# Attention's first batch: the order of the split of x, the masks, the out bias and the weight splits

## The chip, the cores and the metric

The kernel runs on one core of one Trainium2 chip. A core has five engines with a queue each: TensorE (PE, matrix products and transposes), VectorE (DVE), ScalarE (ACT), GpSimd (POOL) and SyncE (SP, which issues transfers here). They meet only at semaphores. The metric is the device time of one execution in microseconds, as the median of several runs.

## The reference

Four layers in a row over x, of shape (8, 512, 512): a stencil, an attention block, a feed-forward block and a gate. Only the attention block bears on the change:

```
scale, shift = split(silu(sin_emb(timestep)) @ W_ada + b_ada)
x = layernorm(src) * (1 + scale) + shift
q, k, v = (x @ Wq + bq), (x @ Wk + bk), (x @ Wv + bv)      # 16 heads of 32
scores = q k^T / sqrt(32) + attention_bias                  # 8 x 16 x 512 x 512
scores = where(src_mask, -inf, scores)
ctx = softmax(scores) @ v
x = x + (ctx @ Wo + bo)
```

All is float32. The attention bias is an input of 134 MB and is read from HBM pair by pair.

## The kernel before

The phases follow each other with a barrier between them: `stencil`, `attention`, `feed_forwards`. In attention a batch is 64 units (`NU`), one per head and block of 128 queries; 16 units (`UC`) make a chunk `c` of four heads, four units with the same queries a group. Each engine has a list written out by hand: first a head for batch 0, then `body`, once for each batch, which walks `u` over the units and says at which unit each side task stands. Nothing reorders the lists.

Precision comes from splits: a float32 tensor is copied to a rounded high part (`...H`, on ACT) and the rest to a low part (`...L`, on DVE), and a product is three matrix products (`split_matmul`, L94 to L98). For the four weight matrices, numbered 0 to 3 (Wq, Wk, Wv, Wo), these are `weights_high(k)` (L872) and `weights_low(k)` (L1135), 128 x 2048 elements each. Staging places are two: Wv comes to the place of Wq (`y`, a shared tile that later holds probabilities) and Wo to that of Wk (the second x). SP issues Wv's load when `s_wl`, the count of low parts, is at least 1, and Wo's at 2, with the bias load of pair 3 behind.

The head of batch 0, engine by engine:

- POOL: identity, loads of the small biases, `power(0)` (var to the power -0.5, L777, then a small product L779), the two halves of the mask (`make_mask`, uint8 to -3e38 or 0, L809), the mask added to bias pairs 0 to 2 (`add_mask`, L815; a pair is two heads of one block, 128 x 1024), and `out_bias` for four row blocks (L798).
- ACT: high parts of weights 0 and 1, `xhat` for four row blocks (L883, waits for the power), `x_high` for four column blocks (L878), `q_high`, `k_high`, high part 2, `copy_v`, the first `exp` (L907), high part 3.
- DVE: statistics, low part 0, the four row blocks times `scale` (L1223) and plus `shift` (L1226), `bq` scaled, `x_low` for four blocks (L1153), low part 1, `q_low`, `k_low`, low part 2, `copy_vT`, two sums of scores (L1180), low part 3.
- PE: four groups of four transposes of x (L992), projections q, k and v ("w" in the code) of chunk 0, the transposition of v, the first four scores (L1046).

PE's results lie in eight banks. `bank_of` gives x two of them in the head, `pS[0]` and `pJ[1]`, in turn, and `first_bank` makes the third and fourth transposition wait for `x_low` of an earlier one (`s_xl`):

```
waits = {("x", 2): (s_xl, 1), ("x", 3): (s_xl, 3), ("k", C): (s_xl, 2), ("w", C): (s_ql, 1), ("v", 0): (s_kl, 1)}
```

In `body`, `exp(u + 1)` and `sum_scores(u + 2)` are issued at unit `u`, and `add_mask` works three pairs ahead. `add_part`, which adds the projected context to x, is the first reader of the out bias's result, in chunk 1. `project_y`, in chunk 1, is the first reader of Wo's parts.

## Time and profile before

| | us |
|---|---|
| median of three runs | 2770.02 |
| lowest, highest | 2769.93, 2770.68 |
| profiled execution | 2768.22 |
| its span | 2766.3 |

PE is busy 2639.3 us of the span, 95%, DVE 1697.8 (61%), ACT 1024.1 (37%), POOL 1025.2 (37%). In the granted clock of PE, 0.981 of 2.4 GHz over the span, the places at half of it are few. Attention begins at 205.5 us of the span and ends near 1190. A row of a timeline says start, duration, engine, line, operation, what is written and read, and in brackets how long the engine was idle before and what ended that. Starts are from the beginning of the span.

### The profile page before, as it was taken

The page shows a single profiled execution, that of the slowest core. Times are in us where ns is not written, and L with a number is a line of the kernel's source. Part 1 is how long each engine was busy: PE and PEld are TensorE (multiplying, and loading weights), DVE is VectorE, ACT ScalarE, POOL GpSimd, SP SyncE. Part 2 cuts the span into 40 slices and gives each one's busy share as a digit, 9 for nine tenths or more (in the row PEclk, how much of TensorE's full clock was granted, in tenths as well). Part 3 has the DMA queues.
Part 4 walks back from the last instruction along what each step waited for, and adds up shares of the span by engine and source line. Part 5 has one row for each costly group of instructions (what it writes and reads, how often), then busy time and mean ns, then how long its engine had stood idle before and what let it go on. Part 6 is the DMA issues. An engine that isn't in the chain of part 4 may idle for free. (4 is left out here: it accounts for less than half of the span.)

```text
span 2766.3 us, 46266 instructions
## 1 busy us (share of the span) xinstructions
PE 2639.3 (95%) x17072; PEld 2037.0 (74%) x17088; DVE 1697.8 (61%) x3341; ACT 1024.1 (37%) x2160; POOL 1025.2 (37%) x756
## 2 busy tenths in 40 slices
PE   7975999999999999969999999999999999999997
PEld 2434777777777777657888888888787887888775
DVE  9976777777777777756444444445554564565443
ACT  1114666666666666611111111111223232322222
POOL 1005677776777777533100110012222322322210
PEclk9997999999999999989999999999999999999998
DMA  4234564655646555531111011103333343244311
GB/s 173 107 132 128 164 194 139 188 154 180 189 144 188 145 185 164 153 105 54 31 31 31 1 31 31 31 1 124 115 103 106 111 134 125 89 130 126 104 46 38
DMA packets 212972, 305.99 MB, mean 111 GB/s; under 512 B 14604, under 2 KB 93516, under 8 KB 210064
## 3 DMA queue, kind: packets, MB, share of 16 engines
q1 hardware_dynamic: 211662, 301.99, 35.3%
q8 instruction: 138, 2.26, 0.3%
q0 software_dynamic: 1088, 1.05, 0.2%
q14 instruction: 84, 0.69, 0.1%
HBM read 268.94 MB, written 34.04 MB: 110 GB/s over the span
## 5 line engine op out<-in xcount | busy, mean ns | idle before, releaser
L815 POOL TENSOR_TENSOR at_bias<-at_bias,at_mask 128x1024 f32<-128x1024 f32 x224 | 483.0, 2160 | 247.3 <-DMA at_bias<-in_fside_Bx16xSxS 245.9
L1180 DVE CUSTOM_DVE_ANT_0 at_bias<-at_bias,at_bank_score 128x512 f32<-128x512 f32 x512 | 338.4, 682 | 186.9 <-PE at_bank_score L1046 140.3
L96 PE MATMUL ff_bank_out<-ff_WH,ff_gH 128*128 128x512 f32 x1024 | 407.9, 398 | 1.9 <-DVE ff_gL L1939 1.9
L96 PE MATMUL ff_bank_hid<-ff_hH,ff_WH 128*128 128x512 f32 x1024 | 402.2, 393 | 2.8 <-DVE ff_WL L1892 2.8
L1667 ACT ACTIVATE ff_g<-ff_bank_hid,ff_b1c 128x512 f32<-128x512 f32 x256 | 175.5, 686 | 607.7 <-PE ff_bank_hid L98 607.7
L98 PE MATMUL ff_bank_out<-ff_WH,ff_gL 128*128 128x512 f32 x1024 | 400.3, 391 | 0.0
L97 PE MATMUL ff_bank_out<-ff_WL,ff_gH 128*128 128x512 f32 x1024 | 399.9, 391 | 0.0
L97 PE MATMUL ff_bank_hid<-ff_hL,ff_WH 128*128 128x512 f32 x1024 | 399.8, 390 | 0.0
L98 PE MATMUL ff_bank_hid<-ff_hH,ff_WL 128*128 128x512 f32 x1024 | 399.7, 390 | 0.0
L1939 DVE TENSOR_TENSOR ff_gL<-ff_g,ff_gH 128x512 fp32r<-128x512 f32 x256 | 178.7, 698 | 348.9 <-ACT ff_g L1667 344.4
L1566 POOL TENSOR_SCALAR ff_WH<-shared 128x1024 fp32r<-128x1024 f32 x144 | 177.1, 1230 | 568.9 <-PE ff_bank_out L98 330.5
L907 ACT ACTIVATE shared<-at_bias,at_nmax 128x512 f32<-128x512 f32 x512 | 366.5, 717 | 17.7 <-DVE at_nmax L1180 17.7
L1053 PE MATMUL at_bank_probT<-at_ident,shared 128*128 128x128 f32 x2048 | 313.8, 280 | 6.1 <-ACT shared L907 6.1
L1053 PEld LDWEIGHTS at_bank_probT<-at_ident,shared 128*128 128x128 f32 x2048 | 228.4, 141 | 94.3 <-issue 67.7
L1937 DVE CAST ff_gH<-ff_g 128x512 fp32r<-128x512 f32 x128 | 72.4, 566 | 359.7 <-ACT ff_g L1667 359.6
L1666 ACT ACTIVATE ff_gH<-ff_bank_hid,ff_b1c 128x512 fp32r<-128x512 f32 x128 | 88.3, 690 | 519.0 <-PE ff_bank_hid L98 519.0
L915 ACT ACTIVATE at_probT<-at_bank_probT 128x512 f32<-128x512 f32 x256 | 152.9, 597 | 269.6 <-PE at_bank_probT L1053 158.4
L96 PEld LDWEIGHTS ff_bank_hid<-ff_hH,ff_WH 128*128 128x128 f32 x1024 | 193.0, 188 | 45.2 <-DVE ff_WL L1892 3.6
L98 PEld LDWEIGHTS ff_bank_out<-ff_WH,ff_gL 128*128 128x128 f32 x1024 | 192.9, 188 | 41.0
L98 PEld LDWEIGHTS ff_bank_hid<-ff_hH,ff_WL 128*128 128x128 f32 x1024 | 192.9, 188 | 40.7
L96 PEld LDWEIGHTS ff_bank_out<-ff_WH,ff_gH 128*128 128x128 f32 x1024 | 193.3, 189 | 39.5 <-DVE ff_gL L1939 2.3
L97 PEld LDWEIGHTS ff_bank_hid<-ff_hL,ff_WH 128*128 128x128 f32 x1024 | 192.9, 188 | 39.6
(310 smaller groups left out, 4282.2 us busy)
## 6 DMA issues: line engine op xcount, KB each, us to landing
at_bias<-in_fside_Bx16xSxS SPq DMA_DIRECT2D x256, 512.0 KB, 3.8
shared<-in_L_cond_Wi SPq DMA_DIRECT2D x128, 256.0 KB, 2.9
shared<-in_L_cond_Wo SPq DMA_DIRECT2D x128, 256.0 KB, 3.0
shared<-x_after_layer SPq DMA_DIRECT2D x64, 256.0 KB, 5.2
st_f<-in_x SPq DMA_DIRECT2D x8, 1024.0 KB, 6.9
x_after_attention<-shared SPq DMA_DIRECT2D x32, 256.0 KB, 2.3
shared<-x_after_attention SPq DMA_DIRECT2D x32, 256.0 KB, 4.4
shared<-in_L_cond_W SPq DMA_DIRECT2D x32, 256.0 KB, 3.0
```

The costliest lines, as they stand in the source:

```text
L96: pe.matmul(out, wh, xh, start=first, stop=False)
L97: pe.matmul(out, wh, xl, start=False, stop=False)
L98: return pe.matmul(out, wl, xh, start=False, stop=last)
L815: pool.tensor_tensor(bias[i % NB][:, :, :], bias[i % NB][:, :, :], mask[:, i // 2 % R, :].unsqueeze(1).to_broadcast([P, 2, S]), ALU.add).t ...
L907: act.activation(prob[u % 2][:, :], bias[u // 2 % NB][:, u % 2, :], ACT.Exp, scale=-1.0, bias=nmax[:, u % 4:u % 4 + 1], accum_out=sums[:, ...
L915: act.activation(probT[g % 2][:, j].rearrange("p k q -> p (k q)"), pT[0][:, :], ACT.Copy).then_inc(s_pt[0], 1)
L1053: t = pe.transpose(pT[u % 2][:, k * P:(k + 1) * P], prob[u % 2][:, k * P:(k + 1) * P], ident[:, :])
L1180: dve.tensor_tensor_reduce(t, t, pS[u % HC][:, :], -1.0, 3.0e38, ALU.add, ALU.min, nmax[:, u % 4:u % 4 + 1]).then_inc(s_max, 1)
L1566: pool.tensor_scalar(WH[:, f, :], stage[f % 2][:, :], 1.0, 0.0, ALU.mult, ALU.add).then_inc(s_wh, 1)
L1666: act.activation(gH[f % 2][:, :], pg[f % 2][:, :], func, bias=column).then_inc(s_gh, 1)
L1667: act.activation(g32[f % 2][:, :], pg[f % 2][:, :], func, bias=column).then_inc(s_g32, 1)
L1939: dve.tensor_tensor(gL[f % 2][:, :], g32[f % 2][:, :], f32(gH[f % 2][:, :]), ALU.subtract).then_inc(s_g, 1)
```

## The change

Only the head and the first batch's body change.

- POOL: only the first half of the mask is made behind the power. Then POOL waits for all of `x_low` (`s_xl` at 4), adds the mask to pairs 0 to 2, and makes the second half. The four `out_bias` of batch 0 go into the body, at units 8, 10, 12 and 14.
- DVE: low part 0 goes behind the `shift` additions, low part 2 from behind `k_low` to ahead of `q_low`, low part 3 into the body at unit 11.
- ACT: high part 2 goes ahead of `q_high`, high part 3 into the body at unit 9.
- PE: the first transposes of x use four banks, `pS[0]`, `pJ[1]`, `pT[0]`, `pT[1]`, and wait for no `x_low`.

```diff
+        first_x = (pS[0], pJ[1], pT[0], pT[1])
+        def x_bank(n, m):
+            return first_x[m] if is_first(n) else bank_of("x", m)
...
             def out_bias(n, slot, r):
                 if r == 0:
+                    pool.wait_ge(s_const, 64)
                     pool.wait_ge(s_xp, n * C + C)
...
             power(0)
-            for half in range(2):
-                make_mask(0, half)
+            make_mask(0, 0)
+            pool.wait_ge(s_xl, C)
             for i in range(3):
                 if i not in ON_PE:
                     add_mask(0, i)
-            pool.wait_ge(s_const, 64)
-            for r in range(R):
-                out_bias(0, 0, r)
+            make_mask(0, 1)
...
+                    if is_first(n) and u in (8, 10, 12, 14):
+                        out_bias(0, 0, (u - 8) // 2)
...
             act.wait_ge(s_const, 64)
+            weights_high(2)
             act.wait_ge(s_bq, 1)
             q_high(0, 0)
             k_high(0, 0)
-            weights_high(2)
             copy_v(0, 0)
             exp(0, 0)
-            weights_high(3)
...
+                    if is_first(n) and u == 9:
+                        weights_high(3)
...
-                waits = {("x", 2): (s_xl, 1), ("x", 3): (s_xl, 3), ("k", C): (s_xl, 2), ("w", C): (s_ql, 1), ("v", 0): (s_kl, 1)}
+                waits = {("k", C): (s_xl, 2), ("w", C): (s_ql, 1), ("v", 0): (s_kl, 1)}
...
             mean_var(0)
-            weights_low(0)
...
+            weights_low(0)
             for m in range(C):
                 x_low(0, 0, m)
             weights_low(1)
+            weights_low(2)
             dve.wait_ge(s_bq, 1)
             q_low(0, 0)
             k_low(0, 0)
-            weights_low(2)
             copy_vT(0, 0)
             sum_scores(0, 0)
             sum_scores(0, 1)
-            weights_low(3)
...
+                    if is_first(n) and u == 11:
+                        weights_low(3)
```

DVE's queue in the head, before (`at_WL` are the low parts of the weights, `shared` the rows of x, `at_xL` the low part of x):

```order
L1135 TENSOR_TENSOR at_WL<-shared,at_WH 128x2048
L1223 TENSOR_TENSOR shared<-shared,at_scale 128x512 x4
L1226 TENSOR_TENSOR shared<-shared,at_shift 128x512 x4
L1228 TENSOR_SCALAR at_bc<-at_bc 128x4
L1153 TENSOR_TENSOR at_xL<-at_bank_score,at_xH 128x512
L1153 TENSOR_TENSOR at_xL<-at_bank_proj,at_xH 128x512
L1153 TENSOR_TENSOR at_xL<-at_bank_score,at_xH 128x512 x2
L1135 TENSOR_TENSOR at_WL<-shared,at_WH 128x2048
L1158 SCALAR_TENSOR_TENSOR at_qL<-at_bank_proj,at_bc,at_qH 128x512
L1164 SCALAR_TENSOR_TENSOR at_kL<-at_bank_proj,at_bc,at_kH 128x512
L1135 TENSOR_TENSOR at_WL<-shared,at_WH 128x2048
L1192 TENSOR_SCALAR at_vT<-at_bank_proj,at_bc 128x512
```

And of the change, whose lines are 5 to 7 further down:

```order
L1229 TENSOR_TENSOR shared<-shared,at_scale 128x512 x4
L1232 TENSOR_TENSOR shared<-shared,at_shift 128x512 x4
L1234 TENSOR_SCALAR at_bc<-at_bc 128x4
L1142 TENSOR_TENSOR at_WL<-shared,at_WH 128x2048
L1160 TENSOR_TENSOR at_xL<-at_bank_score,at_xH 128x512
L1160 TENSOR_TENSOR at_xL<-at_bank_proj,at_xH 128x512
L1160 TENSOR_TENSOR at_xL<-at_bank_probT,at_xH 128x512 x2
L1142 TENSOR_TENSOR at_WL<-shared,at_WH 128x2048 x2
L1165 SCALAR_TENSOR_TENSOR at_qL<-at_bank_proj,at_bc,at_qH 128x512
L1171 SCALAR_TENSOR_TENSOR at_kL<-at_bank_proj,at_bc,at_kH 128x512
L1199 TENSOR_SCALAR at_vT<-at_bank_proj,at_bc 128x512
```

The first low part moved behind the rows of x, the third ahead of q's and k's.

ACT's queue from the first rows of x to its first exps, before (`at_WH` are the high parts of the weights, L907 the exps):

```order
L883 ACTIVATE shared<-shared,at_mrstd,at_rstd 128x512 x4
L878 ACTIVATE at_xH<-at_bank_score 128x512
L878 ACTIVATE at_xH<-at_bank_proj 128x512
L878 ACTIVATE at_xH<-at_bank_score 128x512 x2
L888 ACTIVATE at_qH<-at_bank_proj,at_bc 128x512
L893 ACTIVATE at_kH<-at_bank_proj,at_bc 128x512
L872 ACTIVATE at_WH<-shared 128x2048
L898 ACTIVATE at_v<-at_bank_proj 128x512
L907 ACTIVATE shared,at_sums<-at_bias,at_nmax 128x512
L872 ACTIVATE at_WH<-shared 128x2048
L907 ACTIVATE shared,at_sums<-at_bias,at_nmax 128x512
```

And of the change:

```order
L889 ACTIVATE shared<-shared,at_mrstd,at_rstd 128x512 x4
L884 ACTIVATE at_xH<-at_bank_score 128x512
L884 ACTIVATE at_xH<-at_bank_proj 128x512
L884 ACTIVATE at_xH<-at_bank_probT 128x512 x2
L878 ACTIVATE at_WH<-shared 128x2048
L894 ACTIVATE at_qH<-at_bank_proj,at_bc 128x512
L899 ACTIVATE at_kH<-at_bank_proj,at_bc 128x512
L904 ACTIVATE at_v<-at_bank_proj 128x512
L913 ACTIVATE shared,at_sums<-at_bias,at_nmax 128x512 x2
```

The third high part stands ahead of q's and k's, and the fourth has left this stretch.

POOL's queue from the power on, before (L809 the halves of the mask, L815 masked pairs, L798 out bias):

```order
L777 TENSOR_TENSOR at_rstd<-at_var,at_mhalf 128x4
L779 TENSOR_TENSOR at_mrstd<-at_mneg,at_rstd 128x4
L809 TENSOR_SCALAR at_mask<-at_m 128x1024 x2
L815 TENSOR_TENSOR at_bias<-at_bias,at_mask 128x1024 x3
L798 TENSOR_TENSOR shared<-shared,at_bob 128x512 x4
L815 TENSOR_TENSOR at_bias<-at_bias,at_mask 128x1024 x10
```

And of the change:

```order
L782 TENSOR_TENSOR at_rstd<-at_var,at_mhalf 128x4
L784 TENSOR_TENSOR at_mrstd<-at_mneg,at_rstd 128x4
L815 TENSOR_SCALAR at_mask<-at_m 128x1024
L821 TENSOR_TENSOR at_bias<-at_bias,at_mask 128x1024 x3
L815 TENSOR_SCALAR at_mask<-at_m 128x1024
L821 TENSOR_TENSOR at_bias<-at_bias,at_mask 128x1024 x5
L804 TENSOR_TENSOR shared<-shared,at_bob 128x512
L821 TENSOR_TENSOR at_bias<-at_bias,at_mask 128x1024
L804 TENSOR_TENSOR shared<-shared,at_bob 128x512
```

The out bias stands between masked pairs of the batch now, and the three first pairs wait for the split of x.

## Rows read from the trace of the kernel before

**Rows 1.** Busy time by stretch: us, per engine, then PE's granted clock, DMA share, GB/s.
```profile
218.00:225.00 7.00, 0.00 (x0) 0.00 (x0) 7.00 (x6) 0.00 (x0) 5.00 (x2) 0.50 0.11 44
...
243.80:248.70 4.90, 4.87 (x12) 3.79 (x12) 0.00 (x0) 0.00 (x0) 1.87 (x1) 0.50 0.00 0
...
340.00:360.00 20.00, 20.00 (x219) 15.32 (x218) 14.87 (x36) 14.33 (x36) 16.33 (x12) 1.00 0.49 155
```

**Rows 2.** Waits, 190 to 300: who waited for whom, us, times, longest.
```profile
PE at_bank_score L992 <- DVE shared L1226: 32.8, 1, 32.8
```

**Rows 3.** Timeline of POOL, the head: start, us, engine, line, operation.
```profile
209.60 2.98 POOL L777 TENSOR_TENSOR at_rstd<-at_var,at_mhalf 128x4 f32<-128x4 f32 x1
...
212.95 1.04 POOL L809 TENSOR_SCALAR at_mask<-at_m 128x1024 bf16<-128x1024 uint8 x1
...
215.40 2.54 POOL L815 TENSOR_TENSOR at_bias<-at_bias,at_mask 128x1024 f32<-128x1024 f32 x1
...
233.03 3.34 POOL L798 TENSOR_TENSOR shared<-shared,at_bob 128x512 f32<-128x512 f32 x1
```

**Rows 4.** Timeline of DVE, the head.
```profile
209.38 2.30 DVE L1135 TENSOR_TENSOR at_WL<-shared,at_WH 128x2048 fp32r<-128x2048 f32 x1 [0.59 <-ACT at_WH L872]
...
215.89 2.60 DVE L1223 TENSOR_TENSOR shared<-shared,at_scale 128x512 f32<-128x512 f32 x1
...
224.67 0.68 DVE L1226 TENSOR_TENSOR shared<-shared,at_shift 128x512 f32<-128x512 f32 x1
```

**Rows 5.** Lines L777, L815, L798 of POOL, all executions: ns min/median/max.
```profile
L777 POOL TENSOR_TENSOR at_rstd<-at_var,at_mhalf x8: 1020/1022/2977, 209.6 to 1003.6; 128x4 f32<-128x4 f32 x8
...
L815 POOL TENSOR_TENSOR at_bias<-at_bias,at_mask x224: 2123/2147/3836, 215.4 to 1169.9; 128x1024 f32<-128x1024 f32 x112
...
L798 POOL TENSOR_TENSOR shared<-shared,at_bob x32: 1284/1295/3344, 231.8 to 1061.5; 128x512 f32<-128x512 f32 x32
```

**Rows 6.** Timeline of ACT, the head.
```profile
209.25 1.89 ACT L872 ACTIVATE at_WH<-shared 128x2048 fp32r<-128x2048 f32 x1
...
212.90 0.81 ACT L883 ACTIVATE shared<-shared,at_mrstd,at_rstd 128x512 f32<-128x512 f32 x1 [1.75 <-POOL at_mrstd L779]
```

**Rows 7.** Transfers issued from 205 to 260: KB each, us from issue to landing.
```profile
shared<-in_L_cond_Wv SPq DMA_DIRECT2D x1, 1024.0 KB, 8.4
...
at_bob<-in_L_cond_bo POOLq DMA_DIRECT2D x1, 256.0 KB, 7.6
...
shared<-in_L_cond_Wo SPq DMA_DIRECT2D x1, 1024.0 KB, 5.2
```

**Rows 8.** Timeline of PE, from the first transposes to the second of probabilities.
```profile
225.50 1.09 PE L992 MATMUL at_bank_score<-at_ident,shared 128*128 128x128 f32 x4 [32.82 <-DVE shared L1226]
226.38 1.06 PE L992 MATMUL at_bank_proj<-at_ident,shared 128*128 128x128 f32 x4
...
231.30 0.78 PE L96 MATMUL at_bank_proj<-at_xH,at_WH 128*128 128x512 f32 x1
...
243.83 0.76 PE L96 MATMUL at_bank_proj<-at_xH,at_WH 128*128 128x512 f32 x1 [4.99 <-DVE at_WL L1135]
...
255.91 1.12 PE L1053 MATMUL at_bank_probT<-at_ident,shared 128*128 128x128 f32 x4 [1.39 <-ACT shared L907]
```

**Rows 9.** Timelines of ACT, POOL, DVE and PE, first batch, units 10 to 16.
```profile
271.32 0.72 ACT L907 ACTIVATE shared<-at_bias,at_nmax 128x512 f32<-128x512 f32 x1
...
272.45 2.15 POOL L815 TENSOR_TENSOR at_bias<-at_bias,at_mask 128x1024 f32<-128x1024 f32 x1 [0.79 <-DMA at_bias<-in_fside_Bx16xSxS]
...
272.63 1.09 PE L1053 MATMUL at_bank_probT<-at_ident,shared 128*128 128x128 f32 x8
...
274.72 0.68 DVE L1180 CUSTOM_DVE_ANT_0 at_bias<-at_bias,at_bank_score 128x512 f32<-128x512 f32 x1
...
277.19 0.71 ACT L907 ACTIVATE shared<-at_bias,at_nmax 128x512 f32<-128x512 f32 x1
...
278.31 0.51 PE L1046 MATMUL at_bank_score<-at_kH,at_qH 32*128 32x512 f32 x4 [1.15 <-ACT shared L923]
```

More of the change, by code:

```diff
@@ L877, in x_high @@
                     wait_count(act, s_wp, (n - 1) * C)
-                act.activation(xH[slot][:, m, :], bank_of("x", m)[:, :], ACT.Copy).then_inc(s_xh, 1)
+                act.activation(xH[slot][:, m, :], x_bank(n, m)[:, :], ACT.Copy).then_inc(s_xh, 1)
             def xhat(n, slot, r):
@@ L1073, in _ @@
             for m in range(C):
-                transpose_x(0, 0, m, first_bank("x", m))
+                transpose_x(0, 0, m, x_bank(0, m))
             for kind in "qkw":
@@ L1152, in x_low @@
                 dve.wait_ge(s_xh, n * C + m + 1)
-                dve.tensor_tensor(xL[slot][:, m, :], bank_of("x", m)[:, :], f32(xH[slot][:, m, :]), ALU.subtract).then_inc(s_xl, 1)
+                dve.tensor_tensor(xL[slot][:, m, :], x_bank(n, m)[:, :], f32(xH[slot][:, m, :]), ALU.subtract).then_inc(s_xl, 1)
             def q_low(n, c):
```

## The prediction

> **What bounds the kernel now.** I read first the busy time by stretch, then what TensorE (PE) waits for, then each engine's rows in time order between the start of attention and its first scores.
>
> In the middle of attention's first batch PE is busy 20.00 of 20 us at full clock [rows 1]: from there on PE sets the pace, and work that starts earlier on PE ends the program earlier. Ahead of it PE stands still. It waits 32.8 us for the last addition of `shift` to x (`L1226`) [rows 2], and another 4.99 us, ahead of v's projection at 243.83, for the third weight split (`L1135`) [rows 8]. In the stretch 218 to 225 VectorE (DVE) is busy for all of 7.00 us and GpSimd (POOL) for 5.00, while PE and ScalarE (ACT) do nothing [rows 1]. So the end of the program hangs on a chain: power on POOL, four normalisations on ACT, eight row operations on DVE, transposes, split of x, projections q, k, v, first scores.
>
> Two things in the chain are dear for a reason that the rows show. The power takes 2.98 us here and 1.02 in the median of its eight executions [rows 3, 5]; the DVE split of the first weights (209.38, 2.30 us) lies over it [rows 4]. And the DVE rows of x take 2.60 us while POOL adds masks at 2.54 a pair, but 0.68 once POOL has finished [rows 3, 4].
>
> **The chain of after, step by step, in the times of this trace.** ACT is the next late one behind the power: `xhat` needs rstd, and ACT is in the second high part until 209.25 + 1.89 = 211.14 [rows 6]. A power of 1.02 ends at 210.62, the small product by about 210.95, so `xhat` starts at 211.1 and not 212.90. That is 1.8 us gained of the 1.96 that the power loses. The four `xhat` come 0.71 apart (each row is 0.81 long with its start overlapped), so DVE gets the first at 211.9 and the last at 214.1.
>
> DVE's eight row operations cost 0.61 each where POOL is silent (the row of 0.68 overlaps the one ahead). The fourth scaling starts when the last `xhat` is there, 214.1; then four shifts: 214.1 + 5 x 0.61 = 217.2. One mask conversion of 1.04 is still ahead of the wait on POOL [rows 3]. It would start at 210.95 if its bytes are there; the trace only says that they are by 212.95. So it costs DVE 0 to 1.0; I take 0.2, because the first scalings wait for `xhat` anyway. The vectors and biases that DVE asks for next are loaded from POOL's queue ahead of 209.60 and land within 7.6 us [rows 3, 7], by 217.2: nothing is added. First transpose at 217.4 against 225.50 [rows 8]: **8.1 us gained**.
>
> Transposes now go to four banks. At half clock four of them took 0.88 us (225.50 to 226.38 [rows 8]), so all four groups end by 217.4 + 3.5 = 220.9 and q can begin; before it was 231.30. Gain at this point 10.4. DVE does weights 0 first (217.4 to 219.7), then the four low parts of x; the last high part is ready about 221.8, its low part by 222.5. q's last step needs that and comes at 224 or later, so the split of x is out of the way; q ends between 223.7 and 226.
>
> Here the change adds **a wait that gates others**. Wv's load waits for weights 0 to be split, which is now at 219.7 instead of 211.7. A load of 1 MB took 8.4 us to land amid four others, and 5.2 with one behind it [rows 7]. I take 5.2, since nothing is under way then: landing at 224.9. On ACT the third high part (1.9, as long as the second [rows 6]) now stands ahead of q and k high, so they are queued behind this load: 224.9 to 226.8. On DVE weights 1 run from 222.4 to 224.7 and weights 2 stand ahead of q and k low.
>
> And the masks come in just here. POOL starts them when the last low part is made, 222.5. Weights 1 hold it off until 224.7, as weights 1 before stretched an addition of the out bias from 1.29 to 3.34 us [rows 3, 5]. Then mask pair 0 ends at about 226.8 and pair 1 starts at once, a moment ahead of weights 2. By the alternation of the 2.60 and 2.54 rows, weights 2 wait until about 228.9 and end at 231.1; q low ends at 231.8, and v's projection, which needs its bank and these weights, starts at **231.9 against 243.83** [rows 8]: 11.9 gained. With the 0.2 of the mask, **11.7**.
>
> The Trainium skill, SBUF — State Buffer, section Who interferes with whom, says that a DVE instruction with two SBUF inputs and a GpSimd instruction that reads SBUF exclude each other for the whole instruction. By that rule weights 2 wait out a whole mask pair and v starts at 231.9; without it they would not, and v would start at 229.8. The trace agrees (2.60 against 0.68).
>
> v's twelve products ran at half clock, busy 4.87 us for twelve [rows 1]; at full clock they would take half. PE idled 4.99 us ahead of them [rows 8] and will idle about 4 now, so I keep half clock: nothing gained, up to 2.4 kept for the range.
>
> **Fourth split inside the batch.** At the head it cost this: ACT's 1.9 between the first and second exp held the second transposition of probabilities, with 1.39 us idle at 255.91 [rows 8], and DVE's 2.3 held the third sum. Gone, PE comes to q's next step right after two transpositions: 1.6 us gained. Inside the batch it is paid again. ACT's next exp before was at 271.32 [rows 9]; with 1.9 in front it is at 273.2 and ends at 273.9; its transposition, the second half of PE's row at 272.63, began near 273.05, so PE loses about 1.1. This stretch has no slack to give it back: at 278.31 PE waits 1.15 us for ACT [rows 9]. DVE's 2.3 stand behind the sum of unit 13 and ahead of a copy and the sum of unit 14. That sum ends at 274.72 + 0.68 and its exp starts at 277.19 [rows 9], 1.8 later, and ACT is 1.1 late itself: 2.9 hide the 2.3. If a mask pair holds the port first, 2.1 more, PE loses 1.5. I take 1.8 for both, ends 1.1 and 4.2 (1.9 + 2.3, nothing hidden). The net of the fourth split is -1.6 + 1.8 = **0.2 lost**.
>
> **Out bias inside the batch.** Four POOL additions of 1.29 at units 8 to 14, each behind a mask pair of 2.15 [rows 3, 5]: POOL waited 0.79 us for the load at the pair of 272.45 [rows 9], so each pair falls 0.5 us back, 2.0 in all, while pairs are made three ahead of their use. Nothing is added; the upper end is 4 x 1.29 = 5.2, if POOL's lag reached the sums. The result is needed a chunk later. At the head it lay beside ACT and DVE work, and nothing waited for it there, so nothing comes back.
>
> **Sum.** -11.7 + 0.2 = -11.5 us. The profiled execution took 2768.2 with its span of 2766.3; its own after is 2756.7. It stands 1.8 under the median of the runs, 2770.02, and the runs are what is compared: 2770.0 - 11.5 = **2758.5**.
>
> **Rivals.** *A, luck at the port and the clock.* The high part is a little early, or mask pair 1 a little late, so weights 2 go ahead and v starts 2.1 earlier; PE's shorter pauses keep full clock in v, 1 to 2 more. For it: the two requests are only 0.1 us apart. Against: each needs its own chance. -11.5 - 2.1 - 1 = -14.6: 2755.4. *B, the load is the bound.* Wv takes 8.4 us as before; high part to 230.0, q and k high, and weights 2 behind mask pair 2: v at about 234.1. Against: the DMA engines are empty then. -9.3: 2760.7; with the fourth split at its dear end -6.9: 2763.1. *C, the batch gives it back.* If the first batch is paced by its bias loads and masks and not by PE, then an early start is waited out: PE's 20.00 of 20 speaks against it; within 2 us of before, 2769. *D, slower.* One mechanism, POOL in the batch: with out bias and the fourth split at the port, masks fall behind and sums stop. Its price is 5.2 for the out bias, 2.3 x 2 for the split's hold-ups of POOL and the pair behind, and 4.2 for the fourth split, 14.0; it decides once this exceeds the 13.3 gained ahead of it: 2770.7, and slower than before by over 0.2% only where more pairs follow late, 2776. Against it: POOL's idle 0.79 us. *E, the power isn't what the weight split slows*, say a first-use cost: then `xhat` starts at 212.9, all shifts by 1.8, 2760.3.
>
> **How the numbers follow.** Forecast with its bounds 0.52, A 0.16, B 0.13, E 0.07, C 0.08, D 0.04. The likeliest time is 2758.5. Leaving out C, D and the far ends of A and B gives 2755.0 to 2763.5. About 0.2% (5.5 us) is what a measurement of this kernel can tell from no change: faster by more is forecast, A, E and nearly all of B, 0.87; within it C, a rest of B and the mild end of D, 0.10; slower the rest of D, 0.03.
>
> **What would show it.** In the profile of after: power near 1.0 us; eight DVE row operations of 0.7; first transpose near 217.4 and four groups in 3.5 us with no wait for x low; third high part on ACT starting near 225 with a DMA as its releaser, q high behind it; third weight split on DVE near 229 to 231; v's projection near 232. Inside the batch: PE waiting about 2 us more between units 10 and 16. Wrong would be: x rows still slow (another cause than POOL), the third high part after 228 (load), or an unchanged time of PE's first batch end though its start moved 11 us (another bound).

## The result, and the profile after

| | before | after |
|---|---|---|
| median of five runs, us | 2770.02 | 2755.15 |
| lowest, highest | 2769.63, 2771.24 | 2753.82, 2758.74 |
| profiled execution | 2768.22 | 2754.93 |
| its span | 2766.3 | 2753.1 |
| granted clock of PE | 0.981 | 0.985 |

The ratio is 0.9948, with an interval of 0.9938 to 0.9959: faster by 0.5%, 14.9 us of the medians against 11.5 forecast. That is inside the range, though only 0.15 above its lower end of 2755.0, and nearer to rival A's 2755.4 than to the likeliest 2758.5; which of the two the trace shows is told below. The engines do the same work in less time. PE's line of the page of after (busy us, share, instructions):

```profile
PE 2635.7 (96%) x17088; PEld 2032.8 (74%) x17088; DVE 1697.2 (62%) x3341; ACT 1024.8 (37%) x2160; POOL 1024.8 (37%) x756
```

Timeline of GpSimd (POOL), after, against [rows 3]; a group "x3" is three instructions in a row:

```profile
209.47 1.04 POOL L782 TENSOR_TENSOR at_rstd<-at_var,at_mhalf 128x4 f32<-128x4 f32 x1
...
211.22 1.04 POOL L815 TENSOR_SCALAR at_mask<-at_m 128x1024 bf16<-128x1024 uint8 x1 [0.42 <-DMA at_m<-in_mask_Bx1xSxS_bk]
222.24 10.35 POOL L821 TENSOR_TENSOR at_bias<-at_bias,at_mask 128x1024 f32<-128x1024 f32 x3 [9.98 <-DVE at_xL L1160]
...
255.62 1.30 POOL L804 TENSOR_TENSOR shared<-shared,at_bob 128x512 f32<-128x512 f32 x1
256.87 2.15 POOL L821 TENSOR_TENSOR at_bias<-at_bias,at_mask 128x1024 f32<-128x1024 f32 x1
258.96 3.33 POOL L804 TENSOR_TENSOR shared<-shared,at_bob 128x512 f32<-128x512 f32 x1
```

The power is 1.04 us (2.98 before). The three masked pairs start when the last low part of x is there and take 10.35 us, not 3 x 2.15: they meet weight splits.

VectorE (DVE), after, against [rows 4]:

```profile
211.82 2.78 DVE L1229 TENSOR_TENSOR shared<-shared,at_scale 128x512 f32<-128x512 f32 x4 [3.17 <-ACT shared L889]
214.52 2.48 DVE L1232 TENSOR_TENSOR shared<-shared,at_shift 128x512 f32<-128x512 f32 x4
...
222.07 2.28 DVE L1142 TENSOR_TENSOR at_WL<-shared,at_WH 128x2048 fp32r<-128x2048 f32 x1
226.72 3.88 DVE L1142 TENSOR_TENSOR at_WL<-shared,at_WH 128x2048 fp32r<-128x2048 f32 x1 [2.37 <-ACT at_WH L878]
...
257.60 3.56 DVE L1142 TENSOR_TENSOR at_WL<-shared,at_WH 128x2048 fp32r<-128x2048 f32 x1
```

Eight row operations take 5.2 us together. The third weight split stands at 226.72 and takes 3.88, the fourth, now in the batch, 3.56: each waits behind a masked pair.

ScalarE (ACT), after:

```profile
224.78 1.92 ACT L878 ACTIVATE at_WH<-shared 128x2048 fp32r<-128x2048 f32 x1 [3.34 <-DMA shared<-in_L_cond_Wv]
226.60 0.67 ACT L894 ACTIVATE at_qH<-at_bank_proj,at_bc 128x512 fp32r<-128x512 f32 x1
```

The third high part waits for Wv's transfer, and q's high part is queued behind it, as the prediction said. PE, after, against [rows 8] and [rows 9]:

```profile
217.15 1.09 PE L999 MATMUL at_bank_score<-at_ident,shared 128*128 128x128 f32 x4 [24.46 <-DVE shared L1232]
...
231.32 0.50 PE L96 MATMUL at_bank_proj<-at_xH,at_WH 128*128 128x512 f32 x1 [3.81 <-DVE at_qL L1165]
...
237.42 0.51 PE L1053 MATMUL at_bank_score<-at_kH,at_qH 32*128 32x512 f32 x4
...
261.91 0.63 PE L1060 MATMUL at_bank_probT<-at_ident,shared 128*128 128x128 f32 x4 [0.96 <-DVE at_probT L1194]
263.89 0.50 PE L1053 MATMUL at_bank_score<-at_kH,at_qH 32*128 32x512 f32 x4 [1.35 <-DVE at_nmax L1187]
```

The first transposes start 8.4 us earlier than at 225.50, v's projection 12.5 earlier than at 243.83, and the scores of unit 14 14.4 earlier than at 278.31 [rows 8, 9]. PE's waits between 190 and 300 (who waited for whom, us, times, longest) show the shorter wait for x, 24.5 instead of 32.8 [rows 2], and two that are new in the batch, the 1.4 and the 1.0:

```profile
PE at_bank_score L999 <- DVE shared L1232: 24.5, 1, 24.5
PE at_bank_proj L96 <- DVE at_qL L1165: 3.8, 1, 3.8
PE at_bank_probT L1060 <- ACT shared L913: 3.4, 3, 1.8
PE at_bank_score L1053 <- DVE at_nmax L1187: 1.4, 1, 1.4
PE at_bank_probT L1060 <- DVE at_probT L1194: 1.0, 1, 1.0
```

### The profile page after: what moved, and what is told of

It reads as the page before. It is cut to its first block and busy times, and to the rows that moved or that the text cites. A ratio compares the mean times of both kernels' runs of the same rounds, so it can differ in the third digit from the quotient of the medians.

```text
span 2753.1 us, 46290 instructions
## 1 busy us (share of the span) xinstructions
PE 2635.7 (96%) x17088; PEld 2032.8 (74%) x17088; DVE 1697.2 (62%) x3341; ACT 1024.8 (37%) x2160; POOL 1024.8 (37%) x756
```

## How the experiments are compared

Single runs of one kernel lie up to 4 or 5 us from their median (the kernel before, over 25 runs: 2764.84 to 2773.95, median 2769.64), so effects of 1 to 2 us are read from the traces. "The port" below is the prediction's name for whatever makes a VectorE instruction with two inputs in SBUF, the core's working memory, and a GpSimd instruction that reads SBUF wait for each other; the runs show that waiting and not the part of the chip behind it. The stencil ahead of attention ends at another time in each trace, by up to 1.6 us; so each trace is shifted until ACT's first weight split (207.44 in before) lies alike. The gains below, in us against before, are of starts in such shifted time: the first transposes of x, the addition of v's bias (DVE, v is ready), and the first transposes of the feed-forward phase, behind all eight batches.

| kernel | first transposes | v ready | end of attention | ratio to before |
|---|---|---|---|---|
| after | 8.2 | 13.1 | 13.7 | 0.9948 |
| p1_power | 1.4 | 1.8 | 1.4 | 0.9995 |
| p2_masks | 6.4 | 5.7 | 5.5 | 0.9977 |
| p3_banks | 0.0 | 3.3 | 3.4 | 0.9986 |
| u_fourth | 8.2 | 13.1 | 12.3 | 0.9950 |
| u_outbias | 8.3 | 13.1 | 12.8 | 0.9941 |
| f_late | 8.3 | 13.1 | 12.8 | 0.9950 |
| m_masks_late | 8.2 | 14.8 | 13.5 | 0.9941 |
| c_fill | 8.3 | 14.7 | 12.4 | 0.9936 |
| c_fill_again | 7.9 | 14.4 | 15.2 | 0.9947 |
| h_best | 7.3 | 17.8 | 18.0 | 0.9933 |
| h_all | 7.3 | 17.8 | 15.8 | 0.9943 |
| h_fill | 7.3 | 17.8 | 15.5 | 0.9935 |

The second and third column repeat within 0.4 between kernels that are alike up to there. The fourth does not: c_fill and c_fill_again are one program, and 2.8 us apart; their section shows where the difference arises. So a difference in it of under 3 us is no verdict, and where one matters below, it is followed along the trace to the place where it arises.

## Experiments: the parts one by one

**p1_power**: before, with the first low part behind the rows of x.

```diff
             mean_var(0)
-            weights_low(0)
             dve.wait_ge(s_ab, 32)
...
+            weights_low(0)
             for m in range(C):
                 x_low(0, 0, m)
```

> The kernel before with one edit: the low part of weights 0 stands behind the additions of shift, so that nothing runs on VectorE beside the power. Masks, out bias, banks and the other splits stay. Theory of the port (VectorE instructions with two inputs in SBUF and GpSimd instructions hold each other off): power 1.0 us as in the whole change, first xhat near 211.0 instead of 212.90; the rows of x still meet the masks at 2.5 us each, so the first transpose comes only 1.8 us earlier, near 223.7, and weights 0 then stand in front of x low, which gives back 0.5 to 1; v's projection near 242.6; 2768.7 us in all. Rival (the first power is slow for a reason of its own): power 3.0, first xhat near 212.9, and the moved split costs its 2.2 us: slower than before, near 2771.

Measured: 2768.52 us, ratio 0.9995 (0.9986 to 1.0005). POOL and DVE of its timeline:

```profile
210.88 1.04 POOL L777 TENSOR_TENSOR at_rstd<-at_var,at_mhalf 128x4 f32<-128x4 f32 x1
...
213.24 7.67 DVE L1222 TENSOR_TENSOR shared<-shared,at_scale 128x512 f32<-128x512 f32 x4 [3.17 <-ACT shared L883]
```

The power is 1.04 us with the mask and everything else as before. That removes rival E: the split of the weights was what slowed it. The four scalings still take 7.67 us, since the masks are still beside them, and the whole is worth 1.4 where 1.8 were expected.

**p2_masks**: before, with masked pairs, second mask half and out bias behind the split of x.

```diff
             power(0)
-            for half in range(2):
-                make_mask(0, half)
+            make_mask(0, 0)
+            pool.wait_ge(s_xl, C)
             for i in range(3):
                 if i not in ON_PE:
                     add_mask(0, i)
+            make_mask(0, 1)
```

> The kernel before with one edit: GpSimd makes only the first half of the mask behind the power, waits for the whole split of x, then adds the masks to pairs 0 to 2, makes the second half and adds the out bias, all still in the head. Theory of the port: power still 2.98 us, but the eight row operations of x on VectorE 0.6 to 1.0 us each, first transpose near 219.0 instead of 225.50; v's projection 4.5 to 6.5 us earlier, near 238 (a mask pair may hold off the third low part); 2764 us. Rival (the rows of x are slow because ACT or the transfers slow them): they stay near 2 us, and the time stays within 1 us of before.

Measured: 2763.87 us, ratio 0.9977 (0.9968 to 0.9987).

```profile
210.51 2.98 POOL L777 TENSOR_TENSOR at_rstd<-at_var,at_mhalf 128x4 f32<-128x4 f32 x1
...
217.37 2.49 DVE L1227 TENSOR_TENSOR shared<-shared,at_shift 128x512 f32<-128x512 f32 x4
...
236.17 2.87 DVE L1136 TENSOR_TENSOR at_WL<-shared,at_WH 128x2048 fp32r<-128x2048 f32 x1 [1.04 <-ACT at_WH L873]
```

The power is slow and the rows of x are fast: the two kinds of slowness have two causes, each removed alone. Of the 6.4 us gained at x, 0.7 go again, most of it in the third split (2.87 instead of 2.29). It starts at 236.17, while POOL makes the second half of the mask (235.87 to 236.91); the three masked pairs are over by then.

**p3_banks**: before, with four banks for the first transposes and without the two waits for `s_xl`. The diff is that of the change.

> The kernel before with one edit: four banks for the first transposes of x, none of which waits for an x low. First transpose unchanged at 225.5, the four groups in 3.5 us, q's projection near 229.0 instead of 231.30, all behind it 2.3 us earlier, 2767.7 us. Rival (q is bound by the low part of x on VectorE, not by the banks): q's last step waits for it, v's projection under 1 us earlier, 2769.5.

Measured: 2765.50 us, ratio 0.9986 (0.9976 to 0.9996), 3.3 gained at v where 2.3 were expected. Only PE's waits change; ACT and DVE read the same results from other banks. q's projection starts at 228.64 in shifted time instead of 231.30, 2.7 earlier, which is what the two waits for `x_low` and the time between them cost. Its first nine products stand 0.43 us apart in before, at half clock, and 0.23 here, but k's projection then waits 1.01 us for the second weight split; the rest of the gain is the balance of those two.

The sum of the three is 7.8 us at x, where the change has 8.2, and 10.8 at v, where it has 13.1. The 2.3 between are what no part has alone: 0.7 is the clock in v's projection, below, and the other 1.6 fall by subtraction to the third high and low part ahead of q's and k's. No run moves these alone, so that share is not shown.

## Experiments: the fourth split and the out bias

**u_fourth**: after, with `weights_high(3)` back behind `exp(0, 0)` and `weights_low(3)` behind the second sum.

> The changed kernel with one part undone: the fourth weight split stands in the head again (high part behind the first exp, low part behind the second sum). From the recorded prediction's sum (1.6 gained at the head, 1.8 lost in the batch): no change within 0.5 us, 2755. From the two traces: second group of scores about 3.3 us later (near 246.1 instead of 242.87), because PE's extra pause also costs the clock, and in the batch 2.1 us come back (scores of unit 14 near 265.0 instead of 263.89): 1.2 us slower than the changed kernel, 2756.3.

Measured: 2755.77 us, ratio 0.9950 (0.9934 to 0.9967). Equal up to v. In the batch its PE waits as before, though the out bias is there:

```profile
265.39 0.51 PE L1052 MATMUL at_bank_score<-at_kH,at_qH 32*128 32x512 f32 x4 [1.15 <-ACT shared L929]
...
268.34 0.66 PE L1059 MATMUL at_bank_probT<-at_ident,shared 128*128 128x128 f32 x4 [0.95 <-ACT shared L913]
```

From the last of the second scores (PE issues them at unit 2) to the scores of unit 14 it takes 18.36 us (before 18.39), after 20.45: the fourth split costs 2.1 in the batch, and the out bias nothing where no split meets it. Unit 14's scores come at 265.05 in shifted time against 264.03: the move is worth 1.0 there, where the prediction had a loss of 0.2. The medians (2755.77 and 2755.15) can't tell so little.

**u_outbias**: after, with the four `out_bias` back in the head, behind the second mask half.

> The changed kernel with one part undone: the four additions of the out bias stand in the head again, behind the second half of the mask. From the recorded prediction (they cost nothing in the batch, as mask pairs are made three ahead): no change within 0.5 us in general, 2755; at most the fourth low part in the batch meets one GpSimd instruction less and PE's waits at units 12 to 14 shrink by up to 1.3 us, 2754. Rival (GpSimd in the batch is short of time): 2 to 5 us faster, 2751.

Measured: 2754.61 us, ratio 0.9941 (0.9928 to 0.9955). The fourth split on DVE:

```profile
260.83 2.63 DVE L1142 TENSOR_TENSOR at_WL<-shared,at_WH 128x2048 fp32r<-128x2048 f32 x1
```

It is 2.63 us, 0.9 shorter, PE's wait of 0.96 is gone, and that of 1.35 stays; the stretch takes 19.66 us instead of 20.45. So in this pair of traces the out bias in the batch costs at most 0.8, by way of the masked pair that the split meets. In after an out bias ends at 256.87 and that pair starts there; its bias had landed at 256.36, so about 0.5 of the 0.9 is the out bias (an estimate from these rows), and the rest is how the pairs happened to lie. With the out bias in the batch and the split at unit 11 the split took 2.94 (h_best) to 3.56 us (after). Unit 14's scores come 1.4 later than in after all the same, since q's step behind the first scores (242.66 to 245.50) ran at half clock in this execution, although PE's list is the same as in after:

```profile
240.00:248.00 8.00, 6.96 (x35) 5.28 (x36) 3.40 (x12) 3.85 (x10) 3.62 (x2) 0.57 0.45 132
```

The columns are us, busy time of PE, weight loads, DVE, ACT and POOL, then PE's granted clock (0.57 here, 1.00 for the same stretch of after), DMA share and GB/s.

**f_late**: after, with the fourth split at units 16 and 17, where I took the exponentials to have more room.

> The changed kernel with one edit: the fourth weight split stands at units 16 (high) and 17 (low) instead of 9 and 11, where PE has projections of chunk 1 and 2 to do. Theory (units 10 to 16 have no slack, each wait of ScalarE or VectorE is one of PE; later PE is the bound): PE's waits of 0.69, 0.96 and 1.35 us at units 11 to 14 shrink to the 1.15 of before at unit 14, and 1 to 2 us are gained, 2753.7. Rival (the split costs PE the same wherever it stands): new waits near unit 18 take the place, 2755.

Measured: 2756.72 us, ratio 0.9950 (0.9937 to 0.9964). This theory fell. PE's waits from 238 to 330:

```profile
PE at_bank_score L1053 <- ACT shared L929: 1.5, 2, 1.1
PE at_bank_score L1053 <- ACT at_pv L929: 1.4, 1, 1.4
PE at_bank_probT L1060 <- DVE at_probT L1194: 1.2, 1, 1.2
```

The low part again takes 3.88 us (267.24), behind a masked pair. The scores of unit 14 come 2.1 earlier than in after, which has 1.35 and 0.96 of such waits. At unit 22 only 0.4 of it is left, which is the split's own price at the new place, and the scores of unit 30, at 293.43, come 1.0 later than in after. The trace shows what was paid there. SP's wait, then the rows of POOL, ACT and PE that hang on it:

```profile
SPq L728 <- DVE at_WL L1142: 5.3, 1, 5.3
...
278.09 2.14 POOL L821 TENSOR_TENSOR at_bias<-at_bias,at_mask 128x1024 f32<-128x1024 f32 x1 [4.41 <-DMA at_bias<-in_fside_Bx16xSxS]
...
291.12 0.82 ACT L889 ACTIVATE shared<-shared,at_mrstd,at_rstd 128x512 f32<-128x512 f32 x1 [1.85 <-POOL at_mrstd L784]
...
293.43 0.50 PE L1053 MATMUL at_bank_score<-at_kH,at_qH 32*128 32x512 f32 x4 [1.42 <-ACT at_pv L929]
```

Wo is staged in the place of the second batch's x, so `load_x` of that batch (L728) waits for the fourth low part. With the part at unit 17 SP stands 5.3 us at this wait, and the bias loads queued behind it are late; a masked pair is late by them, and behind it the power of the second batch (289.78 instead of 288.33 in after), `xhat`, the copy of the context and PE's scores. After and h_best have no such wait of SP, h_all has it with 5.1 us.

## Experiments: the port and the clock at v

**m_masks_late**: after, with one wait changed, so that POOL stays away until three weight splits are done.

```diff
             make_mask(0, 0)
-            pool.wait_ge(s_xl, C)
+            pool.wait_ge(s_wl, 3)
```

> The changed kernel with one edit: GpSimd waits for the third low part of the weights, not for the split of x, before it adds the masks of pairs 0 to 2. It tests the term of the sum by which a mask pair holds the third low part off (3.88 us at 226.72 in the changed kernel). Theory of the port: the third low part takes 2.3 us, from 226.7 to 229.0, v's projection starts near 229.8 instead of 231.32, and PE is 1.5 us ahead or more, if its clock stays up, when the first scores of chunk 1 come; 2753.3 us. Rival (v waits for q's low part and the load in any case): v's projection stays near 231.3, 2755.

Measured: 2753.46 us, ratio 0.9941 (0.9927 to 0.9954).

```profile
227.91 2.29 DVE L1142 TENSOR_TENSOR at_WL<-shared,at_WH 128x2048 fp32r<-128x2048 f32 x1 [2.39 <-ACT at_WH L878]
...
230.92 0.79 PE L96 MATMUL at_bank_proj<-at_xH,at_WH 128*128 128x512 f32 x1 [2.25 <-DVE at_qL L1165]
```

The third split is 2.29 us instead of 3.88, and v's projection starts 1.6 earlier, at 229.85 in shifted time: the port's price as expected. At unit 14's scores 0.6 of it is left, at the next scores nothing. Busy time by stretch says where it went (columns as above). Of m_masks_late:

```profile
240.00:248.00 8.00, 7.95 (x48) 5.85 (x46) 4.25 (x11) 4.86 (x14) 3.38 (x2) 0.79 0.43 133
260.00:268.00 8.00, 5.93 (x63) 4.11 (x61) 6.26 (x13) 3.67 (x10) 8.00 (x4) 0.80 0.55 171
```

The same stretches of after:

```profile
240.00:248.00 8.00, 7.77 (x53) 6.05 (x54) 5.77 (x16) 6.38 (x17) 3.29 (x2) 1.00 0.48 139
260.00:268.00 8.00, 4.73 (x81) 3.51 (x81) 7.19 (x17) 4.40 (x11) 8.00 (x5) 1.00 0.48 150
```

Both stretches are at full clock in after and partly at half here, and PE is at least as busy with fewer instructions: 48 and 63 against 53 and 81.

**c_fill**: after, with 14 products of 128x512 that nobody reads between the projections of k and v, into a bank that is free there. They are extra work, and they fill PE's pause of 3.81 us.

```diff
             for kind in "qkw":
+                if kind == "w":
+                    for _ in range(14):
+                        pe.matmul(pT[0][:, :], WH[:, 0, 0, 0:P], xH[0][:, 0, :], start=True, stop=True)
```

> The changed kernel with work added that nobody reads: between the projections of k and v, where PE idles 3.81 us, 14 products of 128x512 (3.2 us at full clock) into a bank that is free then. It tests whether the clock is what v's projection and the steps behind it pay for PE's pause. Theory: v's projection still starts near 231.3 (at most 0.3 later) but runs at full clock, 2.8 us for the twelve products instead of 4.6, so the first scores come 1.5 us earlier; 2753.6 us. Rival (the half clock at 231.6 to 235.0 comes from elsewhere): v takes 4.6 us as before, 2755.

Measured: 2754.11 us, ratio 0.9936 (0.9922 to 0.9949).

```profile
232.88 0.50 PE L96 MATMUL at_bank_proj<-at_xH,at_WH 128*128 128x512 f32 x1 [0.66 <-DVE at_qL L1168]
```

Its stretches:

```profile
240.00:248.00 8.00, 7.77 (x44) 5.61 (x44) 4.25 (x13) 4.86 (x15) 3.17 (x2) 0.79 0.44 133
260.00:268.00 8.00, 5.70 (x62) 4.18 (x61) 6.59 (x11) 3.21 (x10) 8.00 (x5) 0.85 0.46 142
```

v starts where it did, its twelve products take 3.0 us instead of 4.6, and v is ready 1.6 earlier: half clock does cost what it seems to. But then the same two stretches as in m_masks_late fall to half clock, behind pauses of PE (0.94 and 1.79 us, then 0.95 and 1.35) that stand in after too, and attention ends 1.3 later than in after. Is that the price of the products, or of this execution?

**c_fill_again**: the same program, a second time.

> The same kernel as c_fill a second time (the changed kernel with 14 products that nobody reads between the projections of k and v), to see whether the stretches at half clock lie where they lay. In c_fill the granted clock was 0.79 from 240 to 248 and 0.85 from 260 to 268 of the span, where the changed kernel without the products had 1.00, and attention ended 12.4 us before that of the kernel before, against 13.7. Theory 1, the place belongs to the program: both stretches are again below 0.9, attention ends within 0.3 of 12.4 ahead, and the median gain is 17 to 18 us against the kernel before only by scatter. Theory 2, the place is a matter of the execution (how far the clock's own count stands when attention begins): the stretches are at 1.00 or lie elsewhere, and attention ends 0.7 or more away from 12.4, at best 15.3 ahead (v's addition was 14.7 ahead, and 0.6 were added behind it in the changed kernel).

Measured: 2753.61 us, ratio 0.9947 (0.9934 to 0.9961).

```profile
240.00:248.00 8.00, 8.00 (x49) 6.37 (x48) 4.42 (x13) 5.03 (x14) 3.34 (x2) 0.81 0.43 133
...
260.00:268.00 8.00, 4.93 (x72) 3.55 (x74) 7.19 (x16) 4.39 (x11) 8.00 (x4) 1.00 0.62 178
```

The first stretch is at half clock again, the second is not, and attention ends 15.2 ahead instead of 12.4. So theory 2 holds for the second stretch, and the first came both times. The 2.8 us between the two ends are not this stretch alone. At the scores behind it the two traces are 1.1 apart, at the last scores of attention 1.6 (12.6 and 14.1 ahead of before), and the other 1.2 arise behind the last scores. Of c_fill:

```profile
1172.00:1182.00 10.00, 5.22 (x16) 3.17 (x16) 3.43 (x5) 0.28 (x1) 1.88 (x2) 0.83 0.21 79
```

Of c_fill_again:

```profile
1172.00:1182.00 10.00, 3.27 (x12) 2.04 (x12) 3.60 (x6) 0.00 (x0) 1.54 (x7) 0.98 0.28 105
```

After has a clock of 0.83 in this place too (1170 to 1180), so c_fill_again's 1.5 over after at the end of attention is mostly made here: at the last scores it is 0.2.

In the runs the slower ones of these two programs have the lower clock: the five spans of c_fill go from 2749.8 at 0.987 to 2755.5 at 0.984. c_fill's profile is of its slowest run and c_fill_again's of its fastest. The clock is not all of the scatter, since f_late's 2754.76 and 2758.05 both have 0.985. The products gain 1.6 and 1.3 us at v, and the stretch 240 to 248 takes them back. That this is the products' doing is not shown: m_masks_late and u_outbias have no such products and fall to half clock there as well (0.79 and 0.57). The two ratios, 0.9936 and 0.9947, leave no gain over after's 0.9948 that could be told from none.

## Experiments: a version that beats both

**h_best**: after, with POOL silent until three splits are done (the first mask half too), and the first low part back ahead of the rows of x, but behind the power.

```diff
             mean_var(0)
+            dve.wait_ge(s_rstd, 2)
+            weights_low(0)
             dve.wait_ge(s_ab, 32)
...
-            weights_low(0)
             for m in range(C):
                 x_low(0, 0, m)
...
-            make_mask(0, 0)
-            pool.wait_ge(s_xl, C)
+            pool.wait_ge(s_wl, 3)
+            make_mask(0, 0)
```

> The changed kernel with two edits: the first low part stands behind the power and ahead of the rows of x, in VectorE's 3 us of waiting, so that the load of Wv goes out near 213 instead of 219; and GpSimd makes and adds no mask until the third low part is made. Theory (the chain from first transpose to v's projection hangs on the load, the high part behind it and the port): power stays 1.04, first transpose 0.5 to 0.8 us later (near 217.8), third high part straight behind the split of x near 222.5, k ends near 229, v's projection near 228.5 to 229.5 against 231.32, at full clock since PE hardly idles; 3 to 4 us gained against the changed kernel, 2751.5. Rival (the load was never the bound, the port alone was): as good as the kernel with late masks alone, v near 229.8, 2753.3.

Measured: 2750.62 us, ratio 0.9933 (0.9919 to 0.9947), its span 2748.1: lower than both kernels in medians, 4.5 us under after's, though the two ratios' intervals overlap (after's is 0.9938 to 0.9959). DVE:

```profile
212.16 2.29 DVE L1142 TENSOR_TENSOR at_WL<-shared,at_WH 128x2048 fp32r<-128x2048 f32 x1 [2.17 <-POOL at_mrstd L784]
...
224.33 4.48 DVE L1142 TENSOR_TENSOR at_WL<-shared,at_WH 128x2048 fp32r<-128x2048 f32 x2
```

PE, from k's projection to the first transposition of probabilities:

```profile
226.76 0.47 PE L96 MATMUL at_bank_proj<-at_xH,at_WH 128*128 128x512 f32 x1 [0.48 <-DVE at_WL L1142]
...
236.82 1.81 PE L1060 MATMUL at_bank_probT<-at_ident,shared 128*128 128x128 f32 x8 [1.78 <-ACT shared L913]
```

The first split fills DVE's wait for `xhat` and makes x 0.9 later, but Wv's load goes out earlier: the third high part no longer waits for it, splits 1 and 2 follow each other at 2.24 each, and PE has no pause between k and v. v is ready 4.7 earlier than in after, far more than these times scatter, and attention ends 4.3 earlier. Of the 4.7, m_masks_late has 1.7 by the late masks alone. The early split adds 3.0: v's projection starts 1.4 earlier, and its twelve products take 3.0 us instead of 4.5, at full clock.

**h_all**: h_best with the fourth split at units 16 and 17.

> The two edits of the kernel before this one and the fourth split at units 16 and 17 together. If the gains are independent, 4.5 to 5.5 us against the changed kernel: 2750. If the fourth split's late place costs as much as its early one, 2751.5.

Measured: 2754.31 us, ratio 0.9943 (0.9929 to 0.9957); attention ends 2.2 later than in h_best. At unit 30 it is already 1.2 behind, as f_late was: SP waits 5.1 us for the fourth low part, and PE 1.43 us for ACT at 291.16. Twice, the later place was no better, and with the same wait.

**h_fill**: h_best with five unread products behind the first scores, in the pause ahead of the first transposition of probabilities.

> The kernel with the early first low part and the late masks, with 5 products of 128x512 that nobody reads behind the first scores, where PE waits 1.8 us for the first exp. Theory: PE's clock stays full through the first two transpositions of probabilities and q's next step (1.81 us for eight transposes and half clock in part of 236 to 242 without them), so the second scores come 1 to 2 us earlier: 2749.3. Rival (the pause is too short to matter, and the half clock comes from the pauses ahead): no change, 2750.6.

Measured: 2753.04 us, ratio 0.9935 (0.9921 to 0.9949). The second scores come 1.6 earlier, as expected, unit 14's 1.1; the end of attention is 2.5 later than in h_best. A stretch of h_fill:

```profile
256.00:272.00 16.00, 13.33 (x134) 10.02 (x132) 10.26 (x24) 7.80 (x21) 14.08 (x8) 0.79 0.61 183
```

The same stretch of h_best:

```profile
256.00:272.00 16.00, 13.36 (x150) 10.22 (x147) 12.59 (x27) 10.49 (x29) 15.31 (x9) 1.00 0.66 207
```

Half clock again, 24 us behind the filled pause: 134 instructions of PE in these 16 us instead of 150. After c_fill_again this may be the execution and not the products; either way the gain of 1.6 isn't in the medians.

## Why the prediction was right, point by point

**The bound** was right: work that starts earlier on PE ends the program earlier. v ready 13.1 earlier is 13.7 at the end of attention and 13.2 in the span. Rival C (the batch gives it back) is out.

**Power and rows of x**: forecast 8.1 gained at the first transposes, measured 8.2. The mechanism, two separate collisions of DVE and POOL, is shown by p1_power and p2_masks. Rival E is out.

**Wv's load and the order behind it**: landing forecast 224.9, ACT's high part started at 224.78; the transfer took 5.4 us against 5.2 taken. Rival B is out.

**v's projection**: forecast 231.9, measured 231.32 (231.46 shifted), and the third split did wait out a masked pair, as m_masks_late shows by its 1.6. The order at the port was as forecast too: pair 0 behind split 1, then pair 1 ahead of split 2. The Trainium skill, SBUF — State Buffer, section Who interferes with whom, has the two exclude each other for the whole instruction; the trace agrees, with 3.88 against 2.29 for the split and 4.12 and 4.19 against 2.13 for the pairs.

**The clock**: counted at nothing, with up to 2.4 kept for the range, and this is the mis-sized term. v's products still ran at 0.66 of full clock over 231 to 236, and took 4.6 us instead of 5.3: 0.7 gained. (The prediction's 4.87 is cut off by its stretch at 248.70; before's twelve end at 249.15.) At full clock they take 3.0 (c_fill). The six products of q's next step, behind the first scores, began at 256.68 in before and took 2.68 us at half clock; in after they began at 241.30 and took 1.57 at full. I had looked for a gain at v only. 1.8 of the 2.8 by which the trace beat the forecast at unit 14 is the clock's, 0.7 is v's earlier start, and 0.3 the fourth split's.

**The fourth split**: forecast 1.6 gained in the head and 1.8 lost in the batch. Measured between the first and the second scores 3.3 gained, of which 1.1 is the clock of q's step, and 2.1 lost in the batch. The net is a gain of 1.0 (u_fourth), and without the clock about nothing, where 0.2 lost was forecast.

**The out bias**: forecast nothing, measured at most 0.8, in one pair of traces, by lengthening the fourth split, which the prediction had only as a bound.

**The sum**: 11.5 forecast; 13.7 at the end of attention, 13.2 in the span, 14.9 between medians. **Rival A** was half right: the clock gave 1.8, within its 1 to 2, though 1.1 of it in q's step and not in v; the port gave nothing, since the order there was as forecast. That the median lies at A's 2755.4 is in part luck: the span's 13.2 alone would give 2756.8. **Rival D** (POOL in the batch) had the right place, and a price of 2.1 instead of 14. The last 1.2 to 1.7 of the medians are within the scatter of the runs (after's five lie from 2753.82 to 2758.74).

**What stays open**: what decides in an execution whether a stretch of attention falls to half clock. c_fill and c_fill_again show that one program has it both ways at 260 to 268 and behind the last scores, and twice the same way at 240 to 248; after and u_outbias, with one list of PE, differ at 240 to 248. Why is not shown. So h_fill's loss is read and not proven, and of h_all's 2.2 the 1.0 that its wait does not explain.

## What to carry to other kernels

Where two engines hold each other off, keep the second one away while the first is on the critical path, and let it wait for the last instruction that would collide (here `s_wl` at 3), not for the first convenient one. That alone brought 1.7 us at v and nothing that could be seen at the end. Order work by what its end sets free: the first weight split looked like filler, but it gates a transfer, and in DVE's wait for `xhat` it makes x 0.9 us later and v, on top of the late masks, 3.0 earlier. The fourth low part gates the loads of the next batch's x, which is why putting it off did not pay. And where the clock can fall, one trace proves no difference of a microsecond or two at the end of a phase: compare stretches that both traces have at full clock, or run the same program twice.

## What the runs showed of the hardware

- A tiny instruction can be held as long as a large one: the power on 128x4 took 2.98 us beside a split of 2.30, and 1.04 without it (p1_power).
- The port holds both sides: a split of 2.29 became 3.88 behind a pair, and pairs of 2.13 became 4.19 behind a split. DVE instructions that read one of PE's result banks were not held: q's low part took 0.74 at 230.53 while a masked pair was under way.
- A mask conversion with one input holds a split too: in p2_masks the split of 2.29 became 2.87 beside a conversion of 1.04 (one case; the ends of POOL's rows are rough).
- Filling a pause of PE with unread products gave full clock behind it (3.0 instead of 4.6 us for twelve products), in both executions. A stretch at half clock followed 5 us later that after has at full clock (0.79 and 0.81 for 240 to 248); two kernels without such products have it as well.
- The same program had the granted clock at 0.85 in one execution and at 1.00 in the other for 260 to 268, and at 0.83 and 0.98 for 1172 to 1182: 1.1 and 1.2 us of the 2.8 between their ends of attention.
- A load of 1 MB landed in 5.4 us where nothing else was under way (after) and in 8.4 us amid four others (before).
